# Two attention tiles scored ahead of the norm turns, and the norms spread into two banks beside the ring

## The reference

```python
h = shift_token(x)                            # half of the features from the token before
q, k, v = jnp.split(h @ wqkv, 3, axis=-1)     # 8 heads of 64
q = l2norm(q) * qs ; k = l2norm(k) * ksc      # t / clip(norm(t), 1e-12), per token and head
q, k = rotary_xpos(q, k)
sim = einsum('bhwid,bhwjd->bhwij', q * 8, look_around(k))   # a window and the one before
attn = softmax(where(mask, -max, sim))
x = x + (attn @ look_around(v)) @ wo
h = layernorm(shift_token(x)) ; a, g = split(h @ w1 + b1)
x = x + (a * gelu(g)) @ w2 + b2
```

## Time and profile before

| | us |
|---|---|
| median of 3 runs | 1432.89 (1427.32 to 1449.03) |
| the profiled execution's own time | 1444.55 |
| its span, first to last instruction | 1442.9 |
| PE busy | 1129.8 (78%) |
| DVE busy | 920.7 (64%) |
| ACT busy | 745.9 (52%) |
| POOL busy | 291.1 (20%) |
| mean granted TensorE clock | 0.872 |

### The profile page before, as it was taken

One profiled execution on the slowest core, in us unless ns is written; L12 is line 12 of the kernel. 1 busy time (PEld: TensorE's weight loads), 2 busy tenths in 40 slices (PEclk: granted clock), 3 DMA queues, 4 the chain that ended last, 5 costly groups with the idle time before them and its releaser, 6 DMA issues. The chain is left out here.

```text
span 1442.9 us, 23317 instructions
## 1 busy us (share of the span) xinstructions
PE 1129.8 (78%) x8682; PEld 623.2 (43%) x8754; DVE 920.7 (64%) x1802; ACT 745.9 (52%) x1672; POOL 291.1 (20%) x228
## 2 busy tenths in 40 slices
PE   5986789678698778867969767886796976797687
PEld 4752353254374244315447325432634731642263
DVE  5548765974454975687444587578745468748764
ACT  1346475466235567438423546653842453845474
POOL 0105211510101511232020241033202033204220
PEclk9689799879869889978986977997897797999799
DMA  6004101400101310130010130023001014003100
GB/s 262 1 1 135 37 2 42 116 17 15 32 1 41 106 27 1 63 109 2 15 32 1 59 99 16 1 83 90 2 15 32 1 59 113 2 0 123 49 17 15
DMA packets 39197, 66.19 MB, mean 46 GB/s; under 512 B 5408, under 2 KB 19232, under 8 KB 37152
## 3 DMA queue, kind: packets, MB, share of 16 engines
q1 hardware_dynamic: 37920, 62.43, 14.2%
q10 hardware_dynamic: 1152, 2.10, 0.4%
HBM read 13.12 MB, written 2.10 MB: 11 GB/s over the span
## 5 line engine op out<-in xcount | busy, mean ns | idle before, releaser
L494 POOL TENSOR_TENSOR qk<-pc,ps_ 128x512 f32<-128x512 f32 x128 | 194.1, 1517 | 582.8 <-DVE ps_ L1044 582.8
L1044 DVE TENSOR_TENSOR ps_<-rot,tab_s 128x512 f32<-128x512 f32 x128 | 172.4, 1347 | 26.5 <-DMA rot<-raw 26.5
L871 ACT ACTIVATE prob<-bank,negb,inv_norm 128x128 f32<-128x128 f32 x256 | 121.7, 587 | 57.5 <-DVE negb L1091 57.5
L510 PE MATMUL bank<-hTz,wb_s 128*128 128x512 f32 x256 | 140.0, 677 | 5.3 <-ACT sq L984 5.3
L980 ACT ACTIVATE raw<-bank,vec_s 128x512 f32<-128x512 f32 x128 | 89.8, 701 | 82.5 <-PE bank L510 50.0
L500 POOL TENSOR_TENSOR prob<-prob,recb 128x512 f32<-128x512 f32 x64 | 66.5, 1040 | 308.2 <-DVE recb L1112 308.2
L1042 DVE TENSOR_TENSOR pc<-raw,tab_s 128x512 f32<-128x512 f32 x128 | 109.2, 853 | 19.4 <-ACT raw L980 19.3
L1089 DVE TENSOR_REDUCE negb<-bank 128x8 f32<-128x1024 f32 x64 | 78.2, 1222 | 51.1 <-PE bank L628 50.5
L877 ACT ACTIVATE prob<-bank,negb,inv_norm 128x128 f32<-128x128 f32 x256 | 105.4, 608 | 0.0
L510 PE MATMUL bank<-hTz,w_s 128*128 128x512 f32 (+1 forms) x192 | 87.8, 602 | 12.2 <-DVE hTz L1132 12.2
L536 PEld LDWEIGHTS bank<-kD,qZ 32*128 32x128 f32 x1024 | 83.0, 249 | 20.5 <-issue 20.5
(11 more groups left out here) (153 smaller groups left out, 2123.9 us busy)
## 6 DMA issues: line engine op xcount, KB each, us to landing
rot<-raw SPq DMA_DIRECT2D x256, 128.0 KB, 2.0
vS<-vB SPq DMA_DIRECT2D x24, 512.0 KB, 4.4
vS<-vB SPq DMA_DIRECT2D x8, 384.0 KB, 5.7
xn_tok<-x SPq DMA_DIRECT2D x5, 512.0 KB, 3.5
tab_s<-tabs SPq DMA_DIRECT2D x1, 2048.0 KB, 21.1
vS<-x SPq DMA_DIRECT2D x4, 512.0 KB, 3.8
out<-vS SPq DMA_DIRECT2D x8, 256.0 KB, 2.4
wb_s<-wb SPq DMA_DIRECT2D x1, 1536.0 KB, 16.7
```

Source lines behind the costliest of these rows:

```text
L494: pool.tensor_tensor(dst, pc[:, j % 2, :], ps_[:, j % 2, :], ALU.add).then_inc(sum_rdy, 1)
L510: mm = pe.matmul(bank[0:m, i % RING, 0:n], lhs, rhs, start=(q == 0), stop=(q == len(parts) - 1))
L871: ins = act.activation(prob[:, t % 2, 0, h, :], s_bank[t % 2][:, 0, h * P:(h + 1) * P], ACT.Exp, bias=negb[:, t % 2, 0, h:h + 1], scale=qu ...
L1044: dve.tensor_tensor(ps_[:, j % 2, :], rot[:, jb % 4, :], st, ALU.mult).then_inc(prod_rdy, 1)
```

## The change

Three things, in both layers of branch B:

- TensorE scores tiles 0 and 1 right after the value products of chunk 1, ahead of `turn_norms(1)`. VectorE takes both tiles' maxima after `norms(1)` and ahead of the scalings. The calls for these two tiles are taken out of `window_attention`.
- The four spreads of chunk 1 go to banks 4 and 6 in turn, by `spread_aside`, in place of four uses of the ring, and are handed over by two new semaphores, `side_full` and `side_free`. The third and fourth spread wait until the scaling two before has read its bank. TensorE waits for all four scalings before the turns of tile 0 (bank 4) and before the scores of tile 4.
- ScalarE's `copy_norms(l, 1)` stands at the head of its `window_attention`, which is the same place in its order as before.

```diff
-    STAGES += [(f"norm{_l}", 4), (f"wo{_l}", 2), ...
+    STAGES += [(f"wo{_l}", 2), ...
...
 window_scores(l, t), tensor engine
                         elif t == 0:
                             for i in range(USE0[f"wo{l}"] - RING, USE0[f"wo{l}"]):
                                 taken(pe, i)
+                            for k in range(4):
+                                pe.wait_ge(sum_rdy, pair(l, 0, k) + 1)
+                            taken(pe, norm_use(l, 0, 3))
+                            pe.wait_ge(sum_rdy, pair(l, 1, B_QK - 1) + 1)
+                        if t == TPC:
+                            pe.wait_ge(side_free, l * 4 + 4)
...
 window_turn(l, t), tensor engine
+                            if t == 0:
+                                pe.wait_ge(side_free, l * 4 + 4)
...
 window_attention(l), tensor engine
-                        window_scores(l, 0)
                         for t in range(TILES):
-                            if t + 1 < TILES:
+                            if 1 < t + 1 < TILES:
                                 window_scores(l, t + 1)
...
+                        def spread_aside():
+                            pe.wait_ge(rt_rdy, l * CHUNKS + 2)
+                            for k in range(4):
+                                if k >= 2:
+                                    pe.wait_ge(side_free, l * 4 + k - 1)
+                                pe.matmul(bank[:, 4 + 2 * (k % 2), :], seln[:, k * P:(k + 1) * P], rT[:, 1, :], start=True,
+                                          stop=True).then_inc(side_full, 1)
...
+                        window_scores(l, 0)
+                        window_scores(l, 1)
                         turn_norms(1)
-                        spread_norms(1, range(4))
+                        spread_aside()
                         window_attention(l)
...
 window_attention(l), scalar engine
+                        copy_norms(l, 1)
                         for t in range(TILES):
...
-                        copy_norms(1)
                         window_attention(l)
...
 window_attention(l), vector engine
-                        window_maxima(l, 0)
                         for t in range(TILES):
-                            if t + 1 < TILES:
+                            if 1 < t + 1 < TILES:
                                 window_maxima(l, t + 1)
...
                         norms(1)
-                        for k in range(4, B_QK):
+                        window_maxima(l, 0)
+                        window_maxima(l, 1)
+                        for k in range(4):
+                            dve.wait_ge(side_full, l * 4 + k + 1)
                             dve.wait_ge(sum_rdy, pair(l, 1, k) + 1)
-                        scale(1, range(4))
+                            z = qk[:, qk_tile(k), cc(1)]
+                            dve.tensor_tensor(z, bank[:, 4 + 2 * (k % 2), :], z, ALU.mult).then_inc(side_free, 1)
                         window_attention(l)
```

More of the change, by code:

```diff
@@ L67 @@
     STAGES += [(f"qk{_l}0", 8)] + [("a_ln_mean", 2)] * (_l == 0) + [(f"v{_l}0", 4), (f"qk{_l}1", 12), (f"v{_l}1", 4)]
-    STAGES += [(f"norm{_l}", 4), (f"wo{_l}", 2), (f"a_hid{_l}0", 2), (f"ln{_l}", 2), (f"a_hid{_l}1", 2),
+    STAGES += [(f"wo{_l}", 2), (f"a_hid{_l}0", 2), (f"ln{_l}", 2), (f"a_hid{_l}1", 2),
                (f"ln{_l}_mean", 2), (f"a_out{_l}", 1), (f"ffn{_l}", 14)]
@@ L89, in norm_use @@
 def norm_use(l, c, k):
-    return USE0[f"norm{l}"] + k if c else USE0[f"qk{l}1"] + 4 + 2 * k + 1
+    assert c == 0
+    return USE0[f"qk{l}1"] + 4 + 2 * k + 1
 def ffn_use(l, c, k):
@@ L223, in program @@
         sums_copied = sem("sums_of_squares_copied")
+        side_full = sem("norms_spread_aside")
+        side_free = sem("keys_scaled_aside")
         sums_turned = sem("sums_of_squares_turned")
@@ L863, in attention, with copy_norms @@
                                 lay(n - 2)
+                    def copy_norms(l, c):
+                        act.wait_ge(rt_full, l * CHUNKS + c + 1)
+                        act.activation(rT[:, c, :], bank[0:24, 6 + c, 0:256].bitcast(BF16), ACT.Copy).then_inc(rt_rdy, 1)
                     def window_probs(l, t):
@@ L966, in _ @@
                     for l in range(LAYERS):
[L967 to L970, removed]
                         for c in range(CHUNKS):
@@ L986, in _ @@
                                 if c and k == 3:
-                                    copy_norms(0)
+                                    copy_norms(l, 0)
                             if l == 0 and c == 0:
```

## The result

The changed kernel takes **1383.7 us** in the median of 4 runs (1382.5 to 1390.4) against 1439.1 for the kernel before (4 runs): a ratio of **0.965**, interval 0.957 to 0.974. The forecast was 1382.5, the range 1366 to 1402.

The account below looks back on a forecast made before the run. A serial chain before the first exponentials, with ScalarE idle 57.5 us in eight places, was taken as the bound; 4 x 6.8 + 4 x 5.8 = 50.4 us off the 1432.89 median gives 1382.5, range 1366 to 1402.

Parts of the forecast that it names:

- The chain from N to the exponentials: From N, the norms' end, engines work one at a time; first exponentials come at N + 9.15, forecast 7.6 us earlier.
- Start of the scores: TensorE's scores of tiles 0 and 1 start after POOL's last add, about 3.2 us ahead of the norms' end.
- One of my own signs: Among the signs to look for: TensorE's turn of the norms comes within 0.5 us of N, the norms' end.
- Clock during the scores: TensorE's early scores in layer 0 likelier at 2.4 GHz; layer 1 gains 7.0 us at that level, 5.0 if not.
- Scalings: VectorE's four key scalings, behind both maxima: 2.48 us as before, plus 0.25 for the ping-pong of two banks.
- Third tile: The third tile's exponentials, while the loop fills, begin 6.8 us earlier in layer 0 and 5.8 in layer 1.
- The sum: Eight attentions: 4 x 6.8 + 4 x 5.8 = 50.4 us, giving 1382.5 from the median of 1432.89.
- Scores that don't move: Rival: something still holds the early scores until N; gain 14 us in all, 1418; chance 0.06.
- The slow loop: Rival: TensorE stays at 1.2 GHz through the steady loop; 90 us slower than now, 1523; chance 0.05.
- A later give-back: Rival: clock stays down one tile more while the loop fills; 18 us lost over eight attentions, 1401; chance 0.05.
- The lower level in every transition: Rival: all early scores run at 1.2 GHz; gain 36.8 us, time 1396; chance 0.14.

Follow-up runs that it names:

- the combination: New kernel with the norms' turn between the scores of tiles 0 and 1 and layer 1's table load ahead of the copy: 1381.9 us, ratio 0.958.

## Why the prediction was right

- **The chain from N to the exponentials.** Right in mechanism and size: removed in all eight places, and taking the order back removes all of the gain but one dropped wait (ratio 1.001 with that wait). That moving both tiles is needed is not shown: tile 0's move alone gives as much.
- **Start of the scores.** Half right. I took POOL's last add for the releaser. In batches 1 and 2 the scores started at N - 2.85 to N - 3.15, as said or nearly, but in both layers of batches 0 and 3 the last copy of values came later, and they started at N - 1.7 to N - 1.8. In the trace of before the two ends were 0.1 us apart (N - 3.27 and N - 3.17 in batch 0, layer 0), and I left the second out. In layer 0 it cost 0.9 us at the first exponentials and nothing at the third tile (N + 10.2 against 10.1). One of my own signs failed by it: the norms' turn came within 0.5 us of N in two places only, and at N + 1.3 to 1.6 in the six others, either because the scores started late or because they ran at the lower level.
- **Clock during the scores.** Right for layer 0 (1.00), and in layer 1 the lower level was met in two places of four.
- **Scalings.** I charged 0.25 us for the ping-pong of two banks. It costs nothing in six places (2.48 us for four, as before) and 0.19 in two (2.67).
- **Third tile.** Forecast 6.8 us earlier in layer 0 and 5.8 in layer 1; measured 7.3 (17.4 to 10.1) and 5.1 (17.6 to 12.5). The term mis-sized is layer 1's, at N + 12.5 where I had N + 11 to 12. The third scores at 3.0 us were in my sum; what was short by 1.0 us was the start: I had the first exponentials at N + 1.6 + 1.28 = 2.9, and they began at N + 3.85, since the copy ended at N + 2.5 and not 1.6. The third scores were thus done at N + 10.2 and not 9.2. The table load is confirmed by taking it away (10.3), at 1.4 us rather than 1.28.
- **The sum.** 50.4 forecast, 48.5 measured after N. The median came out within 1.2 us of the forecast partly by luck: the same new kernel had a median of 1392.7 when it ran once more beside the combination, and the level of the kernel before was 1437 to 1440 rather than 1432.9. From 1439.1 the 48.5 us lead to 1390.6; the other 7 that the medians show lie where nothing was changed. By the ratio, 0.965, against my 0.965 (1382.5 / 1432.9), the size is right.
- **Rivals.** Scores that don't move: refuted by the rows. The slow loop: refuted, the loop runs at 1.00 after 163. A later give-back happened, not in the loop but at its tail, 1.2 us in two places of eight. The lower level in every transition: no.

## What to carry to other kernels

Where a chain of short steps on different engines precedes a long stage, look for what the stage's first iterations really need; here four scaled key tiles stood in front of four attention tiles that use none of them. Move the work that needs nothing, give the chain buffers outside the ones that work takes, and then read what each engine has queued in front of its first useful instruction: a copy, a turn or a table load that was free in idle time is now on the path. When run times of one kernel spread more than the effect, measure from a mark that both kernels pass in the same way, and up to a mark that lies ahead of any stretch in which the clock comes and goes.

## What was not expected of the hardware

- Executions of one kernel differ with where the granted clock falls: in two of the new kernel the 50 us from 60 on stood at 0.90 and 0.78, and all work ahead of the first N took 153.3 and 159.4 us.
- A tail of the same work took 9.4 us at a granted clock of 1.00, 10.6 at 0.72 and 11.3 at 0.50. Eight extra products left it fallen in two tails of eight, as many as in the new kernel without them, and cost 0.9 us in each of the others.
- A table load of 1.28 us right behind a copy delayed the exponential by 1.4 us, since the load waits for the copy's end, which the exponential does not.
